# Attention and feed-forward block: every probability unit of query tiles 2 to 7 turned outside TensorE, in pairs, with new instruction orders

## The chip, the cores and the metric

One core of a Trainium2 chip runs the whole program in one launch. The metric is the device time of an execution in microseconds, lower is better. The engines are PE (TensorE, matrix products), DVE (VectorE), ACT (ScalarE), POOL (GpSimd) and SP (SyncE, which here issues all bulk transfers from one queue in order).

## The reference

The input x is 1024 tokens of 512 numbers, all in fp32.

```python
x = x + layernorm(attention(layernorm(x)))
x = x + layernorm(ffn(layernorm(x)))
# attention: 32 query heads, 8 key/value heads of 128, causal, 4 query heads to a key/value head
scores = einsum('bskgd,btkd->bkgst', qh, kh) / sqrt(128); probs = softmax(where(causal, scores, min))
attn = einsum('bkgst,btkd->bskgd', probs, vh);  return attn @ w_dense.T
# ffn: 512 -> 1792 -> 512, silu(g) * u, with activations and weights scaled in blocks of 128
```

## The kernel before

**Precision.** Each fp32 operand of a product is split into a high and a low part (fp32r); `split_passes` gives three passes, high x high, high x low, low x high. The high part is a rounding copy, mostly on ScalarE; the low part is a subtraction, on VectorE or POOL (`lo_part`, `low`).

**Stages.** Values, keys and queries come first (to some 245 us), with the products of two heads at a time in a seven-product scheme (`quad`), and go to scratch in HBM (`k_scr`, `q_scr`, `v_scr`). Then the attention: 8 groups (one key/value head each) of 8 query tiles, so 64 steps t. The order of tiles in a group is 3, 7, 2, 6, 1, 5, 0, 4, so even steps are short tiles (0 to 3) and odd steps long ones (4 to 7). The four query heads are regrouped into four units of 128 rows, each unit holding 32 positions of every head; unit u of tile i sees i * 128 + 32 * (u + 1) keys. Last comes the feed-forward part.

**One step of the attention.** For each unit: scores on PE into one of two PSUM slots (`scores`, item S), scaled and masked maximum on VectorE (`masked_max`, S there), exponential with its sum on ScalarE (`exponentials`, E), reciprocal of the sum on VectorE (`inverse_sum`, E), normalisation on POOL (`norm_head`, E). Then the probabilities have to be turned, keys to the partitions. There are two ways:
- on PE: 128x128 transposes into PSUM (`turn_probs`, item P, line L1920), the high part by ScalarE and the low part by VectorE, both out of PSUM;
- by exchange (`swaps`): SyncE stores a unit in `p_scr` (`swap_away`) and loads it back with its 32-row bands regrouped (`swap_back`, four loads for each unit, in place, all but parts that need not move), VectorE turns 32x32 squares into a buffer `square` (`turn_squares`, T), ScalarE takes the high part and VectorE the low part (H; for unit 3 of tile 7 POOL takes it, HP). Both read SBUF. A unit that goes this way computes its scores with the keys in quarters (runs of 32 keys), for the whole diagonal block, less one block of the upper quarters for units 0 and 1.

Exchanged are, at odd steps 3 to 55, units 1, 2 and 3 of tiles 4, 5 and 6 and all units of tile 7: 87 units. All else is turned on PE.

Then weighted values (`weighted_values`, PV, 3 passes for each block of 128 keys) into one PSUM bank, its high and low part (O, on ScalarE and VectorE), the output share of the group (`output_share`, Y, 12 matmuls) and its addition (A, VectorE). The first weighted sum of a tile waits for all its turned units. Long tiles have one buffer of turned probabilities (`pT`) and one of rows (`probs_long`), short ones likewise (`pT_short`, `probs_short`). `hi_of_swap` waits for the weighted sums of the long tile before.

**What sets the order.** Every engine runs in program order and meets the others at semaphores. The order of the attention's items is written out by `step_items` and `pair_items` and then shifted engine by engine by the tables PE_MOVES, ACT_MOVES, DVE_MOVES, POOL_MOVES and the ..._LATER tables. The queue on SyncE has its own loop; an item in it that waits holds all behind it.

Of the kernel before, what the change touches and what calls it, by code (L numbers as in the profile page):

```python
# [5 lines left out]
F32 = mybir.dt.float32  # L6
# [5 lines left out]
P = 128  # L12
# [8 lines left out]
def sandwich_kernel(nc, x, w_v, w_qk, w_dense, w_up, w_down, s_up, s_down, out):  # L21
# [81 lines left out]

    def low_number(t, u, on_pool):
        units = [w for w in swaps(t) if (w in POOL_LOW[TILES[t]]) == on_pool]
        return low_count(t - 2, on_pool) + units.index(u) + 1

    def low_count(t, on_pool):
        return sum((u in POOL_LOW[TILES[k]]) == on_pool for k in SWAPPED if k <= t for u in swaps(k))

    def step_items(t):
        s, g, items, following, two = t % NT, t // NT, [], t < T - 1, p_banks(t) == 2
        last = g == G - 1
        if t == 0:
            shares = [[], [], [], []]
        elif not two:
            shares = [[], [0], [1], [2, 3]]
        else:
            shares = [[], [0], [1], []] if following else [[], [0, 1], [], [2]]

        if t == T - NT:
            items.append(("zeros",))
        exps = [("E", t + 1, h) for h in range(HG) if following and not swapped(t + 1, h)]
        for h in range(HG):
            items.append(("P", t, 0, h))
            if following and not swapped(t + 1, h):
                items.append(("S", t + 1, h))
            if h >= 1:
                items += exps[:1]
                del exps[:1]  # L130
            items += [("Y", t - 1, head) for head in shares[h]]
            if t == 0 and h == 2:
                items.append(("RQ", 2))
            if t == 1 and h == 0:
                items.append(("RQ", 3))
            if h == 2 and T - NT <= t < T - 2:
                items.append(("RQ", t + 2))
            if not last and s in (4, 5) and h % 2:
                items.append(("RKV", g + 1, (s - 4) * 2 + h // 2))

        if t == 1:
            return items + [("P", t, 1, 0), *exps, ("Y", t - 1, 2), ("P", t, 1, 1), ("Y", t - 1, 3), ("P", t, 1, 2),
                            ("P", t, 1, 3), ("A", t - 1),
                            *[("S", 3, u) for u in swaps(3)]]
        if two:
            if following:
                items += [("P", t, 1, 0), *exps, ("Y", t - 1, 2), ("P", t, 1, 1), ("Y", t - 1, 3),
                          ("P", t, 1, 2), ("PV", t, 0), ("P", t, 1, 3), ("PV", t, 1)]
            else:
                items += [("P", t, 1, 0), ("Y", t - 1, 3), ("P", t, 1, 1), ("P", t, 1, 2), ("PV", t, 0), ("PV", t, 1),  # L150
                          ("P", t, 1, 3)]
        items += exps if not two else []
        if t >= 1:
            items.append(("A", t - 1))
# [1948 lines left out]
```

## Time and profile before

| | |
|---|---|
| runs | 1141.95, 1142.47, 1142.70 us; median 1142.47 |
| profiled execution, first to last instruction (span) | 1140.7 us |
| mean granted TensorE clock | 0.996 |
| runs' median less that span | 1.8 us |
| busy: PE, DVE, POOL, ACT | 1122.7, 833.9, 713.9, 626.1 us |

The profile gives no time of the profiled execution but its span; the runs' median is set against that. Mean durations of single instructions that the prediction uses beside the rows below, in ns: maximum on VectorE of 1024 columns 1219 (896: 1075, 768: 954, 640: 814), its reciprocal 157, its low part out of PSUM of 512 columns 680 (384: 545, 256: 416, 128: 270); on ScalarE the exponential of 1024 columns 1153, the high part out of PSUM of 512 columns 585 (384: 470, 256: 370, 128: 255), out of `square` 1048 for 1024 columns, 939, 839 and 721 for 896, 768 and 640, the query copy of 512 columns with 32-column runs (L1253) 619 and the plain copy `up_hi` 617; on VectorE the squares of 1024, 896, 768 and 640 columns 1233, 1101, 971 and 832 and the low parts out of `square` 1294, 1077, 969 and 914.

How to read it: the busy share of an engine is an average over stages with different limits, so a change is judged in its own stage. The records of some matmuls are missing: 562 of the 582 transposes of the attention are in the trace.

### The profile page before, as it was taken

How to read it: one execution, taken by the hardware profiler on the slowest of the kernel's cores; microseconds unless marked ns; L12 is line 12 of the kernel's file. 1: busy time of each engine (PE TensorE's matmuls, PEld its weight loads, DVE VectorE, ACT ScalarE, POOL GpSimd, SP SyncE). 2: the span in 40 equal slices, each digit the busy share in tenths (PEclk: the TensorE clock that was granted, in tenths of full speed). 3: DMA queues.
4: the chain of work that ended last, by engine and by line, in shares of the span. 5: the costliest groups of instructions: out<-in, count | busy, mean ns of one | idle time of the engine just before them, and what ended most of it. 6: DMA issues, size and time to landing. Idle time of an engine off the chain costs nothing.

```text
span 1140.7 us, 17840 instructions
## 1 busy us (share of the span) xinstructions
PE 1122.7 (98%) x5512; PEld 945.5 (83%) x5512; DVE 833.9 (73%) x1987; ACT 626.1 (55%) x1350; POOL 713.9 (63%) x802
## 2 busy tenths in 40 slices
PE   8999999999999999999999999999999989999997
PEld 7888888888888888888888888888887768888885
DVE  5645454557888898888888888988579766666666
ACT  6532324237776767676767767776588532222224
POOL 7844447436674865856757748567784746665645
PEclk9999999999999999999999999999999999999999
DMA  6443555335466475485474665754410033333422
GB/s 224 138 158 148 184 203 185 148 128 183 129 194 218 152 224 183 142 265 173 143 262 127 206 205 159 240 172 121 167 65 1 20 115 114 109 111 92 121 65 98
DMA packets 154696, 173.76 MB, mean 152 GB/s; under 512 B 41776, under 2 KB 128496, under 8 KB 151280
## 3 DMA queue, kind: packets, MB, share of 16 engines
q1 hardware_dynamic: 154608, 172.68, 46.8%
q8 instruction: 43, 0.70, 0.2%
q14 instruction: 45, 0.37, 0.1%
HBM read 101.06 MB, written 71.57 MB: 151 GB/s over the span
## 4 chain that ended last, share of the span: by engine, by line
PE 93%; DVE 2%; POOL 2%; ACT 1%; issue 1%; DMA 0%; POOLq 0%; DVEq 0%; SPq 0%; ACTq 0%
PE psS L1813 29%; PE psOY L1942 17%; PE psOY L1957 15%; PE psOY L1813 15%; PE psT L1813 11%; PE psT L1920 5%; POOL x L1100 0%; DVE pT_lo L1468 0%; PE psS L1819 0%; POOL raw_up L1000 0%; DMA raw<-in_w_v 0%; DVE y L1612 0%; POOL rstd L1031 0%; POOL up_lo L896 0%; DVE probs_long L1533 0%
## 5 line engine op out<-in xcount | busy, mean ns | idle before, releaser
L955 POOL TENSOR_SCALAR probs_long<-probs_long,rsum 128x896 f32<-128x896 f32 (+9 forms) x124 | 129.0, 1042 | 62.3 <-DVE rsum L1539 60.9
L1269 ACT ACTIVATE probs_long<-probs_long,negmax 128x896 f32<-128x896 f32 (+9 forms) x124 | 121.4, 979 | 42.0 <-DVE negmax L1533 39.7
L955 POOL TENSOR_SCALAR probs_short<-probs_short,rsum 128x416 f32<-128x416 f32 (+15 forms) x128 | 69.0, 543 | 120.1 <-DVE rsum L1539 119.7
L1813 PE MATMUL psS<-kT_hi,qT_hi 128*128 128x256 f32 (+8 forms) x384 | 133.0, 346 | 0.0
L1813 PE MATMUL psS<-kT_hi,qT_lo 128*128 128x256 f32 (+8 forms) x384 | 128.3, 334 | 0.0
L1813 PE MATMUL psS<-kT_lo,qT_hi 128*128 128x256 f32 (+8 forms) x384 | 128.1, 334 | 0.0
L1957 PE MATMUL psOY<-wd_hi,oT_hi 128*128 128x512 f32 x256 | 106.8, 417 | 3.3 <-DVE oT_lo L1468 3.3
L1022 POOL TENSOR_SCALAR hidden<-mask,hr,hs 128x128 f32<-128x128 f32 x112 | 50.0, 456 | 86.2 <-DVE hr L1632 82.1
L1957 PE MATMUL psOY<-wd_hi,oT_lo 128*128 128x512 f32 x256 | 101.2, 395 | 0.0
L1957 PE MATMUL psOY<-wd_lo,oT_hi 128*128 128x512 f32 x256 | 100.5, 393 | 0.0
L1264 ACT CAST pT_hi<-square 128x1024 fp32r<-128x1024 f32 (+3 forms) x87 | 77.6, 892 | 31.6 <-DVE square L1552 31.2
L1942 PE MATMUL psOY<-pT_hi,v_hi 128*128 128x512 f32 x222 | 92.3, 416 | 0.6 <-DVE pT_lo L1468 0.6
L1306 ACT ACTIVATE mask<-psS 128x256 f32<-128x256 f32 x56 | 21.5, 383 | 129.0 <-PE psS L1813 128.9
L1552 DVE STREAM_TRANSPOSE square<-probs_long 128x1024 f32<-128x1024 f32 (+3 forms) x87 | 90.6, 1041 | 0.0
L1813 PE MATMUL psS<-up_hi,xn1T_hi 128*128 128x512 f32 x224 | 88.3, 394 | 2.0 <-DVE xn1T_lo L1468 1.9
L896 POOL TENSOR_TENSOR qT_lo<-q_raw,qT_hi 128x512 fp32r<-128x512 f32 x64 | 82.8, 1294 | 11.5 <-ACT qT_hi L1253 11.5
L1468 DVE TENSOR_TENSOR pT_lo<-square,pT_hi 128x896 fp32r<-128x896 f32 (+3 forms) x81 | 85.4, 1055 | 3.7 <-ACT pT_hi L1264 2.4
L1813 PE MATMUL psS<-up_hi,xn1T_lo 128*128 128x512 f32 x224 | 87.9, 393 | 0.0
L1813 PE MATMUL psS<-up_lo,xn1T_hi 128*128 128x512 f32 x224 | 87.7, 392 | 0.0
L1942 PE MATMUL psOY<-pT_hi,v_lo 128*128 128x512 f32 x222 | 87.2, 393 | 0.0
L1942 PE MATMUL psOY<-pT_lo,v_hi 128*128 128x512 f32 x222 | 86.8, 391 | 0.0
L1533 DVE CUSTOM_DVE_ANT_0 probs_long<-psS,mask 128x1024 f32<-128x1024 f32 (+9 forms) x82 | 83.8, 1024 | 3.2 <-PE psS L1813 2.5
(200 smaller groups left out, 3267.1 us busy)
## 6 DMA issues: line engine op xcount, KB each, us to landing
q_raw<-q_scr SPq DMA_DIRECT2D x64, 256.0 KB, 3.4
p_scr<-probs_long SPq DMA_DIRECT2D x24, 512.0 KB, 3.3
raw<-in_w_qk SPq DMA_DIRECT2D x10, 1024.0 KB, 5.6
p_scr<-probs_long SPq DMA_DIRECT2D x21, 448.0 KB, 2.5
probs_long<-p_scr SPq DMA_DIRECT2D x90, 96.0 KB, 2.8
q_scr<-cB SPq DMA_DIRECT2D x16, 512.0 KB, 2.6
q_scr<-cA SPq DMA_DIRECT2D x16, 512.0 KB, 2.7
raw_wd<-in_w_dense SPq DMA_DIRECT2D x8, 1024.0 KB, 8.4
```

The lines of the kernel that those rows point to most:

```text
L896: return nc.gpsimd.tensor_tensor(dst, source, hi.bitcast(F32), ALU.subtract)
L955: nc.gpsimd.tensor_scalar(row, row, rsum[:, column(t, h)], 1.0, ALU.mult, ALU.mult).then_inc(p_ready, 1)
L1022: last = nc.gpsimd.tensor_scalar(to, columns_of(h_sb[:, m % 2, b * P:(b + 1) * P], to), hr[:, m % 2, b:b + 1], hs[:, m % 2, b:b + 1], ALU. ...
L1264: nc.scalar.copy(pT[0][:, 0:TILES[t] + 1, u * P:(u + 1) * P], squared(t, u)).then_inc(done, 1)
L1269: nc.scalar.activation(row, row, ACT.Exp, bias=negmax[:, column(t, h)], scale=-1.0, accum_out=lsum[:, column(t, h)]).then_inc(e_done, 1)
L1468: return nc.vector.tensor_tensor(dst, source, hi.bitcast(F32), ALU.subtract)
L1533: nc.vector.tensor_tensor_reduce(out=out, in0=scores, in1=keys, scale=-SCALE, scalar=-NEG, op0=ALU.add, op1=ALU.min, accum_out=negmax[:, c ...
L1552: nc.vector.transpose(square[u][:, 0:m * P].rearrange("p (k a q) -> p a k q", k=m, a=HG), whole_row(t, u).rearrange("p (a k x) -> p a k x" ...
L1813: last = nc.tensor.matmul(dst, a, b, start=(start and k == 0), stop=(stop and k == len(terms) - 1), skip_group_check=resumed)
L1920: last = nc.tensor.transpose(bank[:, (j % TPB) * P:(j % TPB + 1) * P], whole_row(t, h)[:, j * P:(j + 1) * P], ident[:])
L1942: last = nc.tensor.matmul(psO, a, b, start=(j == 0 and k == 0), stop=(j == i and k == 2))
L1957: last = nc.tensor.matmul(psY, a, b, start=(h == 0 and k == 0), stop=(h == HG - 1 and k == 2))
```

## The change

1. **More is exchanged.** At all steps 3 to 55, all four units of tiles 2 to 7 are exchanged (156 units); only tiles 0 and 1, and the steps outside that range, are turned on PE. There several units share one turn item (`HEADS`: all four units of tile 0, two of tile 1).
2. **Pairs.** Two units (`PACKS`) lie interleaved in one row and are stored, loaded back (four loads for a pair), turned (in place in `squares`) and rounded by ScalarE together. Loads go to buffers of their own, `squares_long` and `squares_short`, and `p_scr` has two halves. A load back waits for the low parts of the tile of the same length before.
3. **Low parts** go by the table `LOWS` to VectorE (0) or POOL (1).
4. **Normalisation** of units 0 and 2 of tiles 6 and 7 goes to ScalarE; reciprocals are taken for two units at once.
5. **Masks**: one `band` for all units.
6. **q_scr** is laid out by tile, so a load of queries takes pieces of 2 KB instead of 512 B, and a store of queries writes pieces of 512 B instead of 4 KB.
7. **New orders**: for each of the five engines one string of letters (`..._WEAVE`) says which kind of item comes next, over the whole attention and the first steps of the feed-forward part.

```diff
-    SWAPPED = range(3, T - NT, 2)
-    SWAPS = {4: (3, 2, 1), 5: (3, 2, 1), 6: (3, 2, 1), 7: (3, 2, 1, 0)}
...
-    POOL_LOW = {4: (), 5: (), 6: (), 7: (3,)}
...
+    AWAY = range(3, T - NT)
+    PACKS = {0: ((0, 1, 2, 3),), 1: ((0, 1, 2, 3),), 2: ((0, 1), (2, 3)), 3: ((0, 1), (2, 3)), 4: ((0, 1), (2, 3)), 5: ((0, 1), (2, 3)), 6: ((0, 1), (2, 3)), 7: ((0, 1), (2, 3))}
+
+    DVE_LOW, POOL_LOW = 0, 1
+    LOWS = {0: (), 1: (), 2: (((0, 1), 0), ((2, 3), 1)), 3: (((0, 1), 0), ((2, 3), 1)), 4: (((0, 1), 0), ((2,), 0), ((3,), 1)), 5: (((0, 1), 0), ((2,), 1), ((3,), 1)), 6: (((0,), 0), ((1,), 1), ((2,), 0), ((3,), 1)), 7: (((0,), 0), ((1,), 1), ((2,), 0), ((3,), 1))}
+
+    SCALED_BY_ACT = {6: (0, 2), 7: (0, 2)}
+
+    STAYING = (0, 1)
+    HEADS = {0: ((0, 1, 2, 3),), 1: ((0, 1), (2, 3)), 2: ((0,), (1,), (2,), (3,)), 3: ((0,), (1,), (2,), (3,)), 4: ((0,), (1,), (2,), (3,)), 5: ((0,), (1,), (2,), (3,)), 6: ((0,), (1,), (2,), (3,)), 7: ((0,), (1,), (2,), (3,))}
+    def away(t):
+        return t in AWAY and TILES[t] not in STAYING
+
+    def length(t):
+        return int(TILES[t] >= TPB)
...
+    SP_WEAVE = ("qqkqqwqoqoiioqqioiwoqqoiipqpjjqooipipqkjjqooiiqqooiioiqqoi"
...
+    PE_WEAVE = ("psppspssvvvvpspsspspypypvpvpsspvsspvsvvsyypspvssvssvyysyyv"
...
+    SP_ITEMS = woven(SP_KINDS, SP_WEAVE)
+    PE_ITEMS = woven(PE_KINDS, PE_WEAVE)
+    ACT_ITEMS = woven(ACT_KINDS, ACT_WEAVE)
+    DVE_ITEMS = woven(DVE_KINDS, DVE_WEAVE)
+    POOL_ITEMS = woven(POOL_KINDS, POOL_WEAVE)
...
-        square = [at(f"square{u}", 116 + 4 * u, [P, S]) for u in range(HG)]
-        masks = [at(f"mask_{u}", (142, 64, 68)[u], [P, HG, 2 * P]) for u in range(HG - 1)]
+        squares = [at("squares_short", 142, [P, HG * BANK]), at("squares_long", 116, [P, HG * S])]
+        band = at("band", 64, [P, 2 * HG - 1, 2 * P])
...
-        q_scr = nc.dram_tensor("q_scr", [G * HG, P, S], F32, kind="Internal").ap()
+        q_scr = nc.dram_tensor("q_scr", [G, P, NT, HG * P], F32, kind="Internal").ap()
-        p_scr = nc.dram_tensor("p_scr", [HG, P, S], F32, kind="Internal").ap()
+        p_scr = [nc.dram_tensor(f"p_scr_{n}", [2, HG // 2, P, 2 * size], F32, kind="Internal").ap()
+                 for n, size in (("short", BANK), ("long", S))]
...
+            if away(t):
+                k = pack_of(t, u)
+                pack = PACKS[TILES[t]][k]
+                rows = pack_rows(probs_of(t), t, k).rearrange("p (c u x) -> p u c x", c=HG, u=len(pack))
+                return rows[:, u - pack[0]]
...
+            def swap_away(t, k):
+                last = PACKS[TILES[t]][k][-1]
+                if scaled_count(t, last, ON_POOL):
+                    sp.wait_ge(p_ready[lane(t)], scaled_count(t, last, ON_POOL))
+                if scaled_count(t, last, ON_ACT):
+                    sp.wait_ge(p_ready_act[lane(t)], scaled_count(t, last, ON_ACT))
+                rows, c, count = pack_rows(probs_of(t), t, k), length(t), pack_count(t, k)
+                if count > 2:
+                    sp.wait_ge(swap_in[c][k], 16 * HG * (count - 2))
+                sp.dma_start(p_scr[c][count % 2, k, :, 0:rows.shape[1]], rows).then_inc(swap_out[c][k], 16)
+
+            def swap_back(t, k):
+                c, rows = length(t), pack_rows(squares[length(t)], t, k)
+                w = rows.shape[1] // HG
+                sp.wait_ge(swap_out[c][k], 16 * pack_count(t, k))
+                earlier, end = previous(t), PACKS[TILES[t]][k][-1] + 1
+                if earlier >= 0:
+                    sp.wait_ge(swap_lo[c], low_count(earlier, DVE_LOW, end))
+                    if low_count(earlier, POOL_LOW, end):
+                        sp.wait_ge(swap_lo_pool[c], low_count(earlier, POOL_LOW, end))
+                for b in range(HG):
+                    sp.dma_start(rows[b * SPAN:(b + 1) * SPAN, :].rearrange("q (a x) -> q a x", a=HG),
+                                 p_scr[c][pack_count(t, k) % 2, k, :, b * w:(b + 1) * w].rearrange("(a q) x -> q a x", a=HG)
+                                 ).then_inc(swap_in[c][k], 16)
+
+            def store(kind, n, tile, done):
+                if kind == "k":
+                    sp.dma_start(k_scr[n], tile[:]).then_inc(done, 16)
+                else:
+                    sp.dma_start(q_scr[n // HG].rearrange("p n (h c) -> p n h c", h=HG)[:, :, n % HG, :],
+                                 tile[:].rearrange("p (n c) -> p n c", n=NT)).then_inc(done, 16)
...
+            def norm_head(t, u):
+                pool.wait_ge(r_done[lane(t)], pair_count(t, u))
+                row = filled_row(t, u)
+                if u < HG - 1 and away(t - 2) and not away(t):
+                    end = (u + 1) * row_slot(t)
+                    nc.gpsimd.memset(probs_of(t)[:, end - SPAN * (HG - 1 - u):end], 0.0).then_inc(const_ready, 1)
+                nc.gpsimd.tensor_scalar(row, row, rsum[:, column(t, u)], 1.0, ALU.mult, ALU.mult).then_inc(p_ready[lane(t)], 1)
+
+            def lo_of_swap(t, units):
+                pool.wait_ge(swap_hi[length(t)], exchange_count(t, pack_of(t, units[-1])))
+                hi, lo = (turned_units(v_, t, units) for v_ in pT_of(t))
+                low(lo, squared(t, units), hi).then_inc(swap_lo_pool[length(t)], 1)
...
+            def hi_of_swap(t, k):
+                units = PACKS[TILES[t]][k]
+                act.wait_ge(swap_turned[length(t)], exchange_count(t, k))
                 act.wait_ge(o_full, t - 1)
+                nc.scalar.copy(turned_units(pT_of(t)[0], t, units), squared(t, units)).then_inc(swap_hi[length(t)], 1)
...
+            def norm_row(t, u):
+                act.wait_ge(r_done[lane(t)], pair_count(t, u))
+                row = filled_row(t, u)
+                nc.scalar.activation(row, row, ACT.Copy, scale=rsum[:, column(t, u)]).then_inc(p_ready_act[lane(t)], 1)
...
+            def turn_squares(t, k):
+                c = length(t)
+                dve.wait_ge(swap_in[c][k], 16 * HG * pack_count(t, k))
+                rows = pack_rows(squares[c], t, k)
+                rows = rows.rearrange("p (b x) -> p b x", x=SPAN)
+                nc.vector.transpose(rows, rows).then_inc(swap_turned[c], 1)
+
+            def lo_of_swap(t, units):
+                dve.wait_ge(swap_hi[length(t)], exchange_count(t, pack_of(t, units[-1])))
+                hi, lo = (turned_units(v_, t, units) for v_ in pT_of(t))
+                lo_part(lo, squared(t, units), hi).then_inc(swap_lo[length(t)], 1)
...
+                def in_quarters(first, last, blocks, at_):
+
+                    dst = bank[:, at_:at_ + (last - first) * SPAN * blocks].rearrange("p (c k x) -> p c k x", c=last - first,
+                                                                                     x=SPAN)
+                    shown = TILES[t] if first == 2 and u < 2 else blocks
+                    return product(dst[:, :, 0:shown], [(queries, [k_[:, 0:blocks * P].rearrange(
+                        "p (k c x) -> p c k x", c=HG, x=SPAN)[:, first:last, 0:shown] for k_ in kT[e]])])
+
+                if away(t) and n > BANK:
+                    in_quarters(0, 2, TILES[t] + 1, BANK - n // 2)
+                    last = in_quarters(2, HG, TILES[t] + 1, BANK)
+                elif away(t):
+                    last = in_quarters(0, HG, max(TILES[t] + 1, 2), 0)
```

In the new lists PE has 288 transposes instead of 582. Around steps 24 and 25 (a tile 3, then a tile 7) they read, with a unit's number or a pair's last:

```
PE:   PV(24,3) S(28,3) S(29,0) S(29,1) Y(24,0) Y(24,1) Y(24,2) Y(24,3) PV(25,0) PV(25,1)
ACT:  N(27,0) E(27,3) H(25,0) N(27,2) O(24) H(25,1) E(28,0)
DVE:  S(28,3) A(23) O(24) L(25,(0)) L(25,(2)) T(26,0)
POOL: N(27,1) N(27,3) L(25,(1)) L(25,(3)) D(4,0)
```

## Rows read from the trace of the kernel before

**Rows 1.** The head of the page: span, busy time and share of each engine.
```profile
span 1140.7 us, 17840 instructions
...
PE 1122.7 (98%) x5512; PEld 945.5 (83%) x5512; DVE 833.9 (73%) x1987; ACT 626.1 (55%) x1350; POOL 713.9 (63%) x802
...
PE   8999999999999999999999999999999989999997
```

**Rows 2.** The page's chain that ended last, by engine and by line.
```profile
PE 93%; DVE 2%; POOL 2%; ACT 1%; issue 1%; DMA 0%; POOLq 0%; DVEq 0%; SPq 0%; ACTq 0%
...
by line: PE psS L1813 28.5%; PE psOY L1942 17.1%; PE psOY L1957 15.3%; PE psOY L1813 15.1%; PE psT L1813 11.2%; PE psT L1920 5.3%; issue 0.7%; POOL x L1100 0.4%; DVE pT_lo L1468 0.4%; PE psS L1819 0.4%; POOL raw_up L1000 0.4%; DMA raw<-in_w
```

**Rows 3.** Stretches: us, busy PE, PEld, DVE, ACT, POOL, clock, DMA share, GB/s.
```profile
479.71:557.75 78.04, 78.04 (x407) 67.15 (x407) 68.23 (x160) 54.99 (x120) 51.90 (x55) 1.00 0.60 191
```

**Rows 4.** PE's waits from 200 to 900 us: total, times, longest.
```profile
PE psOY L1957 <- DVE oT_lo L1468: 3.3, 3, 2.5
PE psOY L1942 <- DVE pT_lo L1468: 0.6, 2, 0.3
```

**Rows 5.** The chain from 479 to 500 us: start, us, what.
```profile
482.55 0.44 PE psT L1920 x4
...
494.48 2.81 PE psOY L1957 x12
```

**Rows 6.** PE's instructions in order of time: start, us, line, operands.
```profile
480.50 0.40 PE L1813 MATMUL psS<-kT_lo,qT_hi 128*128 128x512 f32 x1
480.73 0.40 PE L1813 MATMUL psS<-kT_hi,qT_lo 128*128 128x512 f32 x1
...
482.39 0.60 PE L1920 MATMUL psT<-ident,probs_short 128*128 128x128 f32 x4
482.74 0.47 PE L1957 MATMUL psOY<-wd_hi,oT_hi 128*128 128x512 f32 x1
483.05 0.39 PE L1957 MATMUL psOY<-wd_lo,oT_hi 128*128 128x512 f32 x1
483.28 0.39 PE L1957 MATMUL psOY<-wd_hi,oT_lo 128*128 128x512 f32 x1
...
497.30 0.34 PE L1813 MATMUL psS<-kT_lo,qT_hi 128*128 128x384 f32 x1
497.48 0.34 PE L1813 MATMUL psS<-kT_hi,qT_lo 128*128 128x384 f32 x1
```

**Rows 7.** Groups by line and shape: count, busy us, mean ns, idle before.
```profile
L1552 DVE STREAM_TRANSPOSE square<-probs_long 128x1024 f32<-128x1024 f32 x24 | 29.6, 1233 | 0.0
L955 POOL TENSOR_SCALAR probs_long<-probs_long,rsum 128x1024 f32<-128x1024 f32 x26 | 29.4, 1129 | 19.6 <-DVE rsum L1539 19.2
...
L1552 DVE STREAM_TRANSPOSE square<-probs_long 128x640 f32<-128x640 f32 x21 | 17.5, 832 | 0.0
...
L896 POOL TENSOR_TENSOR pT_lo<-square,pT_hi 128x1024 fp32r<-128x1024 f32 x6 | 14.5, 2417 | 10.2 <-ACT pT_hi L1264 10.2
```

**Rows 8.** Instructions of POOL, then of VectorE, around 500 us.
```profile
497.31 2.43 POOL L896 TENSOR_TENSOR pT_lo<-square,pT_hi 128x1024 fp32r<-128x1024 f32 x1 [1.71 <-ACT pT_hi L1264]
499.69 1.52 POOL L955 TENSOR_SCALAR probs_short<-probs_short,rsum 128x320 f32<-128x320 f32 x1
...
499.33 1.49 DVE L1468 TENSOR_TENSOR pT_lo<-square,pT_hi 128x1024 fp32r<-128x1024 f32 x1
...
504.65 2.42 DVE L1468 TENSOR_TENSOR pT_lo<-square,pT_hi 128x1024 fp32r<-128x1024 f32 x2
```

**Rows 9.** The groups of the head's copy that waits for its store.
```profile
L1368 ACT COPY cA<-psT 128x512 f32<-128x512 f32 x20 | 11.7, 587 | 43.0 <-PE psT L1813 40.6 <-DMA q_scr<-cA 2.4
```

**Rows 10.** Transfers from 479.71 to 557.75 us: queue share, size, landing.
```profile
q1 hardware_dynamic: 13242, 14.80, 60.0%
...
p_scr<-probs_long SPq DMA_DIRECT2D x4, 512.0 KB, 3.1
...
raw_wd<-in_w_dense SPq DMA_DIRECT2D x1, 1024.0 KB, 8.2
```

More of the change, by code:

```diff
@@ L104, in low_number @@
[L104 to L154, printed above, removed]
-        if t == 0:
-            items.append(("mask",))
-        if last:
-            if not following:
-                items.append(("X", 0))
-        elif s in (4, 6):
-            items.append(("D", g + 1, (s - 4) // 2))
-        items += [("PV", t, j) for j in range(2 if two else 0, TILES[t] + 1)]
-        items.append(("O", t))
-        return items
@@ new lines, in sandwich_kernel @@
+    PLACE = {item: k for units in SOFT for k, item in enumerate(units)}
+    TURNS = [(t, b, heads) for t in range(T) if not away(t) for b in range(TILES[t] // TPB + 1)
+             for heads in HEADS[TILES[t]]]
+    EXCHANGED = [[(t, k) for t in AWAY if away(t) and length(t) == c for k in range(len(PACKS[TILES[t]]))] for c in range(2)]
+    LOW_PARTS = [[[(t, units) for t in AWAY if away(t) and length(t) == c for units, engine in LOWS[TILES[t]] if engine == e]
+                  for e in range(2)] for c in range(2)]
@@ L274, in sandwich_kernel @@
+    ON_ACT = [[(t, u) for t, u in units if away(t) and u in SCALED_BY_ACT.get(TILES[t], ())] for units in SOFT]
+    ON_POOL = [[item for item in units if item not in done] for units, done in zip(SOFT, ON_ACT)]
+    TURN = {("P", *item): k for k, item in enumerate(TURNS)}
     T_ATT = len(TURN)
     assert T_ATT % 2 == 0
[L276 to L277 removed]
@@ L507, in softmax_count, with previous, items, each @@
-    def softmax_count(t, h):
-        return SOFT[t, h] + 1
+    def previous(t):
+        return max((k for k in AWAY if k < t and away(k) and length(k) == length(t)), default=-1)
+    def items(kind, arguments):
+        return [(kind, *args) for args in arguments]
+    def each(kind, count):
+        return [(kind, n) for n in range(count)]
+    QUERIES, PIECES_LATER = range(2, T), [(g, piece) for g in range(1, G) for piece in range(PIECES_KV)]
+    BLOCKS = [(t, j) for t in range(T) for j in range(TILES[t] + 1)]
@@ new lines, in scaled_count, with exchange_count, pack_count, low_count @@
+    def scaled_count(t, u, members):
+        return sum(PLACE[item] <= PLACE[t, u] for item in members[lane(t)])
+    def exchange_count(t, k):
+        return EXCHANGED[length(t)].index((t, k)) + 1
+    def pack_count(t, k):
+        return sum(pack == k and tile <= t for tile, pack in EXCHANGED[length(t)])
+    def low_count(t, engine, before=HG):
+        return sum(tile < t or tile == t and units[0] < before for tile, units in LOW_PARTS[length(t)][engine])
+    def pack_of(t, u):
+        return [u in pack for pack in PACKS[TILES[t]]].index(True)
@@ new lines, in filled_row, with column, score_bank, squared @@
+        def filled_row(t, u):
+            return whole_row(t, u) if away(t) else whole_row(t, u)[:, 0:keys_of(t, u)]
+        def column(t, u, count=1):
+            first = 2 * HG * lane(t) + PLACE[t, u] % (2 * HG)
+            return slice(first, first + count)
+        def score_bank(t, u):
+            return psT[:, PLACE[t, u] % 2, :] if lane(t) else psS[:, PLACE[t, u] % 2, :]
+        def squared(t, units):
+            k = pack_of(t, units[-1])
+            pack = PACKS[TILES[t]][k]
+            blocks = pack_rows(squares[length(t)], t, k).rearrange("p (a u k q) -> p u k a q", a=HG, u=len(pack), q=SPAN)
+            return blocks[:, units[0] - pack[0]:units[-1] + 1 - pack[0]]
```

479 lines of the change are left out of this document (213 added, 266 removed), and 232 rows, old and new, of tables (ACT_LATER, ACT_MOVES, ACT_NORMS, DVE_LATER).

## The prediction

> **What bounds the kernel now.** I read four views, coarse to fine. The head of the page [rows 1] gives the span, 1140.7 us, with PE busy for 98% of it, and PE stands at nine tenths or more in nearly every slice; no other engine passes 73%. The chain of waits shared out by line [rows 2] says the same from the end backwards: 93% of it is PE, and 5.3% of the span is line L1920, the turning of probabilities on TensorE. The stretches [rows 3] show one whole group of the attention, 478 to 558 us, eight query tiles in 78.1 us: PE is busy for all of it at full granted clock, VectorE for 68.2, POOL for 51.9, ScalarE for 55.0. PE's own waits from 200 to 900 us [rows 4] are under 5 us together, and most of that lies after the attention, where the feed-forward begins. So in the attention an instruction taken off PE shortens the program by its own length, until another engine or a transfer is late.
>
> **Prices on PE.** A matmul's "us" in the trace overlaps the next one, so I price by distance from start to start. The chain counts 0.44 us for four turns [rows 5]; the start times say why [rows 6]: 0.35 until the next matmul starts, and this one holds the next back 0.31 where 0.23 is usual. I take 0.108 a turn. A matmul of 512 columns costs 0.231 (three of the output share take 0.69), one of 384 contiguous columns 0.173: 0.455 ns a column. Scores in quarters (runs of 32 keys apart) cost 0.236 at 512 columns: 0.464 ns.
>
> **What PE loses and gains.** Removed: unit 0 of tiles 4, 5 and 6 (7 tiles of each kind between t = 3 and 55, with 5, 6 and 7 blocks: 126 turns) and all four units of tiles 2 and 3 (6 of each, 3 and 4 blocks: 168). 294 turns x 0.108 = 31.8 us. Added: an exchanged unit needs its whole diagonal block. Unit 0 of tiles 4 to 6 goes from 96 missing columns to 64 not shown, so 32 more, x 21 = 672; tiles 2 and 3 get 96+64+32 = 192 more each, x 12 = 2304. 2976 columns x 3 passes x 0.455 = 4.1 us. 36,288 columns change from contiguous to quarters: x 3 x 0.009 ns = 1.0 us. Net **26.7 us**, or 4.7 for a whole group: 73.4 instead of 78.1. Nothing else on PE changes in number; weighted sums and output shares stay.
>
> **What the others must do in 73.4 us**, for one group, from [rows 3, 7] and the durations in the profile section.
> VectorE: turns' low parts go (three long unit 0s 3.3, short ones 4 x (0.545+0.68) = 4.9: -8.2). Squares come: 0.83+0.97+1.10 for the long ones, and from the slope of the rows (1.04 ns a column, 0.16 for the start) 0.56 and 0.70 x 4 for the short ones: +8.0; twelve instructions fewer through pairs, -2.0. Low parts: of 28 units 18 stay here, 11.9 us against 12.8. Sixteen reciprocals fewer, -2.5; wider maxima, +0.8. Together -4.8: 63.4 us, 86%.
> POOL: normalisations of units 0 and 2 of tiles 6 and 7 leave, -4.3; wider rows +0.6; its low parts, 2.417 us for 1024 columns, grow from one unit to ten: 1.5 (tile 4), 3.6 (tile 5), 4.2 (tile 6), 2.4 more (tile 7), 4.2 (tiles 2 and 3): +16.0. 64.2 us, 87% instead of 67%. This is the largest shift of the change.
> ScalarE: high parts out of PSUM -7.1, out of squares +6.9, pairs -2.1, four normalisations +4.1, wider exponentials +0.6: 57.4 us, 78%.
> No one exceeds PE's 73.4, and each has over 9 us of air, against 9.8 on VectorE today. Where squares are turned in place, where ScalarE copies them through runs of 32, and for the band mask, I take today's price. The trace bounds that: query copies of 512 columns with such runs take 619 ns, plain ones 617, so the price is nought, at worst the 0.16 start again for each.
>
> **What is late next.** The lengths of the new lists on PE, priced as above, give the air of each exchange. From the last score of a long tile to its first weighted sum stood 20 to 25 us of other PE work, now 25 (tile 7) to 31 (tile 6); for short tiles 26 and more. The pair's chain is longer: for tile 7 maximum 1.2, exponential 1.15, reciprocal 0.16, normalisation 1.13, out 1 MB 5.6, back 1 MB 5.6 (the page has 5.6 for 1 MB of query weights; half a MB takes 3.1 in rows 10), squares 2.3, high part 1.9, low part 2.4 = 21.5 of 24.9. Tile 5: 18.5 of 26. They fit.
> Tighter is the end of it, where engines stand in order. For tile 7 ScalarE's list reads: output of the tile before, then the high part of the second pair. On PE lie between that output and the first weighted sum one score of tile 1 (0.35), two of tile 5 (1.95) and four output shares (2.8): 5.1 us. Needed are 0.59 (output copy), 1.93 (pair of 1024), VectorE's low part of unit 2 (1.2) and POOL's of unit 3 (2.42), plus 0.1 for handing over. If the two low parts can't run together that is 6.2: 1.1 to 1.2 late. Whether they can the trace shows [rows 8]: POOL's low part ends at 499.74, VectorE's, started at 499.33, takes 1.49 instead of 1.2 (two of them took 2.42), and POOL's next, a normalisation of 320 columns that should take 0.54, takes 1.52 and ends 0.4 after VectorE's. So one waits for the other. Six such tiles: 6.9 us.
> The Trainium skill states this as a rule ("SBUF — State Buffer", section "SBUF: two separate sides"): GpSimd and a VectorE instruction with two SBUF inputs hold the shared port pair in turn, for a whole instruction, and the other fully blocks. The trace agrees; it speaks against the change, for low parts that read PSUM become low parts that read SBUF twice.
> At the other places the order leaves something: after the output of tile 1 come 3.9 us for VectorE's output low part and the pair's low part of tile 5 (1.3+1.9), before tile 3 stand 2.5 us for the output alone (1.3). The output's low part had 1.7 us before its share in the old order and made PE wait 3.3 us in all [rows 4]; it has 1.8 to 3.5 now.
> Before and after: storing queries in pieces of 512 B makes 16 heads' stores slower than 2.7 us, and ScalarE waited 2.4 us for them already [rows 9]; but the copy that waits has 4 us until PE needs its bank, so I cost it nought (at worst 32 x 1 us if that cover were gone). Loading queries in pieces of 2 KB only gets quicker. The new order after tile 55 keeps its instructions apart from joined turns; nought, plus or minus 2 us, by the 3.2 us that PE waits there.
>
> **The sum.** 1140.7 - 26.7 + 6.9 = 1120.9 us of span. The runs' median, 1142.5, lies 1.8 above the profiled span, so the forecast is **1122.7 us**.
>
> **Rivals.**
> (a) No stall: the low parts find their gaps, as they did everywhere today (no PE wait in the groups). For it: rows 4, and what is late once moves the rest later. Then 1142.5 - 26.7 = 1115.8.
> (b) VectorE and POOL become the bound through their common port. In today's group (478 to 558 us) five POOL instructions beside one of VectorE's 12 low parts took 0.5 to 1.0 longer than alone, 3.7 us together (the 320 columns of rows 8 are the first), at 67% load on POOL; at 87%, with POOL instructions of up to 2.4 us, a VectorE low part that finds POOL at work waits 1.2 on average. If half of that (0.6) arrives at PE for each of the 27 long tiles: 16 us, 1131.8. Against it: 9 us of air on each.
> The rule of the skill named above would give this case if the order didn't keep the two apart.
> (c) The other side: the exchange is late. A group's transfers [rows 10] grow from 14.8 MB at 60% to 21.3 MB (28 units out, and whole units back, instead of 13 out and seven eighths back); at today's price a byte that is 0.60 x 21.3/14.8 x 78.0/73.4 = 92%. Pieces of twice the length make it less; how much no row shows for this pattern. Queues lengthen the landings: the 1 MB of dense weights takes 8.2 in this stretch. Tile 7 has 3.4 us to spare over two landings; beyond 7.3 each PE waits, and beyond 9.5 each six tiles eat the 26.7. At 10 each: (20 - 11.2 - 3.4) x 6 = 32, so 1148. On SyncE's queue each load back also stands behind stores that wait for POOL.
>
> **Chances.** Forecast 0.37 (its own range 1119 to 1127), (a) 0.27, (b) 0.20, (c) 0.11, something between (b) and (c) 0.05. Range 1112 to 1139: it holds (a), (b) and half of what is between. A difference of 0.2%, 2.3 us, is about what can be told from none. Faster 0.84, same 0.04, slower 0.12.
>
> **What would show it.** Right: turns on L1920 fall from 582 to 288 in the program and its share of the chain from 5.3% to under 3%; a group takes 73.4 to 75 us; PE idles only before the first weighted sum of tile 7, released by POOL's or VectorE's low part; POOL is busy for 64 us or a little more of it, DMA between 75 and 92%. Wrong: PE waits at many tiles (b), landings over 7 us and PE waits behind squares (c), or a group length under 73, which would mean that a turn costs more than 0.108.

## The result: slower by 56 us, and the profile after

The changed kernel takes 1198.39 us (median of 4 runs, 1194.44 to 1199.78), the kernel before 1142.59 beside it: a ratio of 1.0482, 95% interval 1.0465 to 1.0499. The forecast of 1122.7 missed by 76 us and the range ended at 1139. The profiled execution spans 1195.7 us.

The page of the changed kernel: head, DMA share in slices, and the chain that ended last by engine and by line. They answer to [rows 1] and [rows 2].
```profile
PE 1117.8 (93%) x5218; PEld 928.2 (78%) x5218; DVE 862.6 (72%) x1698; ACT 640.3 (54%) x1237; POOL 804.1 (67%) x836
...
PE 54%; DMA 17%; DVE 13%; issue 5%; POOL 4%; ACT 3%; SPq 3%; DVEq 0%; POOLq 0%; ACTq 0%
PE psS L1586 16%; PE psOY L1586 14%; PE psT L1586 11%; DMA squares_long<-p_scr_long 10%; PE psOY L1719 7%; DMA p_scr_long<-probs_long 6%; PE psOY L1734 5%; DVE pT_lo L1242 4%; SPq L497 2%; DVE squares_long L1329 2%; PE psT L1700 2%; POOL pT_lo L662 1%; DVE probs_long L1310 1%; POOL probs_long L722 1%; DVE y L1387 1%
```
Two things show here. PE has 294 matmuls fewer, as forecast, and the chain is no longer PE's: 46% of it is transfers, VectorE and others. (All turns are in both traces, 582 before and 288 now. The 562 named in the section on the profile before leave out 20 that read `probs_mid`.) No engine is above 72% but PE.

Two stretches of one group each (columns as in [rows 3]): 85.7 and 85.8 us, where the old order took 78.1 and 73.4 were forecast.
```profile
345.83:431.53 85.70, 78.75 (x370) 65.50 (x368) 71.53 (x122) 59.02 (x107) 66.97 (x61) 0.98 0.87 255
431.53:517.32 85.79, 77.34 (x354) 64.09 (x354) 71.17 (x121) 56.47 (x103) 66.49 (x62) 0.96 0.84 248
```
The transfers of the first of them (queue: packets, MB, share; then size and landing); they answer to [rows 10].
```profile
q1 hardware_dynamic: 10318, 21.80, 86.5%
...
squares_long<-p_scr_long SPq DMA_DIRECT2D x8, 256.0 KB, 7.2
q_raw<-q_scr SPq DMA_DIRECT2D x8, 256.0 KB, 6.5
p_scr_long<-probs_long SPq DMA_DIRECT2D x2, 1024.0 KB, 7.6
...
raw_wd<-in_w_dense SPq DMA_DIRECT2D x1, 1024.0 KB, 8.8
```
What waited for what from 250 to 930 us: total, times, longest. The two waits of PE in [rows 4] made 3.9 us together:
```profile
DVE squares_long L1329 <- DMA squares_long<-p_scr_long: 62.9, 37, 3.7
PE psS L1586 <- DVE negmax L1310: 40.3, 20, 4.7
PEld psS L1586 <- issue: 34.0, 14, 4.9
PEld psS L1586 <- DVE negmax L1310: 16.8, 18, 2.1
PEld psOY L1734 <- DVE oT_lo L1242: 13.3, 14, 3.0
```
(PEld is the loading of weights on TensorE. Its rows tell much of the same idle time again and aren't to be added: before the score at 443.88 PE idles 2.75 us for negmax, and its weight load 2.93 us as "issue".) PE hardly waits for turned probabilities: by the same view 2.7 us for POOL's low parts and 0.6 for VectorE's. It waits for the masked maximum (negmax), that is for a free score bank: VectorE, which must free the bank, stands in its list behind squares that haven't landed. The chain shows the link (start, us, what), one for each group:
```profile
422.88 7.10 DMA p_scr_long<-probs_long
...
431.53 9.58 DMA squares_long<-p_scr_long
441.13 1.89 DVE squares_long L1329
...
446.39 3.40 DVE pT_lo L1242
```
At that place, VectorE's instructions, then POOL's, then PE's in order of time:
```profile
436.87 2.31 DVE L1329 STREAM_TRANSPOSE squares_long<-squares_long 128x2048 f32<-128x2048 f32 x1 [3.10 <-DMA squares_long<-p_scr_long]
...
441.13 2.31 DVE L1329 STREAM_TRANSPOSE squares_long<-squares_long 128x2048 f32<-128x2048 f32 x1 [1.45 <-DMA squares_long<-p_scr_long]
443.37 0.35 DVE L1310 CUSTOM_DVE_ANT_0 probs_short<-psS,mask 128x224 f32<-128x224 f32 x1
...
445.26 4.54 DVE L1242 TENSOR_TENSOR pT_lo<-squares_long,pT_hi 128x1024 fp32r<-128x1024 f32 x2
...
445.47 3.24 POOL L662 TENSOR_TENSOR pT_lo<-squares_long,pT_hi 128x1024 fp32r<-128x1024 f32 x1 [0.20 <-ACT pT_hi L1031]
...
443.88 0.42 PE L1586 MATMUL psS<-kT_hi,qT_hi 128*128 128x384 f32 x1 [2.75 <-DVE negmax L1310]
...
446.86 0.63 PE L1734 MATMUL psOY<-wd_hi,oT_hi 128*128 128x512 f32 x1
447.28 0.63 PE L1734 MATMUL psOY<-wd_lo,oT_hi 128*128 128x512 f32 x1
...
448.14 0.40 PE L1734 MATMUL psOY<-wd_hi,oT_hi 128*128 128x512 f32 x1
448.38 0.40 PE L1734 MATMUL psOY<-wd_lo,oT_hi 128*128 128x512 f32 x1
```
VectorE idles 3.10 and then 1.45 us for the two pairs of tile 7; the small maximum at 443.37 comes only after the second, and PE starts at 443.88 after 2.75 us of nothing. Then two low parts of 1024 columns take 4.54 us on VectorE, beside one of 3.24 on POOL (2.417 in [rows 7]). The last lines, of TensorE's clock, are read in the last section.

So two suspects stand: the transfers (rival c of the prediction) and the port that VectorE and POOL share (rival b). Before the experiments the first was the theory (called T), the second the rival (E, the engines), with the in-order lists (O) as a third.

### The profile page after: what moved, and what is told of

It is laid out like the page before. It is cut to its first block, busy times and chain, and to the rows that moved or that the text cites. A ratio compares the mean times of both kernels' runs of the same rounds, so it can differ in the third digit from the quotient of the medians.

```text
span 1195.7 us, 16875 instructions
## 1 busy us (share of the span) xinstructions
PE 1117.8 (93%) x5218; PEld 928.2 (78%) x5218; DVE 862.6 (72%) x1698; ACT 640.3 (54%) x1237; POOL 804.1 (67%) x836
## 4 chain that ended last, share of the span: by engine, by line
PE 54%; DMA 17%; DVE 13%; issue 5%; POOL 4%; ACT 3%; SPq 3%; DVEq 0%; POOLq 0%; ACTq 0%
PE psS L1586 16%; PE psOY L1586 14%; PE psT L1586 11%; DMA squares_long<-p_scr_long 10%; PE psOY L1719 7%; DMA p_scr_long<-probs_long 6%; PE psOY L1734 5%; DVE pT_lo L1242 4%; SPq L497 2%; DVE squares_long L1329 2%; PE psT L1700 2%; POOL pT_lo L662 1%; DVE probs_long L1310 1%; POOL probs_long L722 1%; DVE y L1387 1%
## 5 line engine op out<-in xcount | busy, mean ns | idle before, releaser
L1586 PE MATMUL psS<-kT_hi,qT_hi 128*128 128x384 f32 (+6 forms) x384 | 140.5, 366 | 40.6 <-DVE negmax L1310 40.3
L1329 DVE STREAM_TRANSPOSE squares_long<-squares_long 128x1792 f32<-128x1792 f32 (+3 forms) x54 | 102.2, 1893 | 62.9 <-DMA squares_long<-p_scr_long 62.9
L722 POOL TENSOR_SCALAR probs_long<-probs_long,rsum 128x768 f32<-128x768 f32 (+9 forms) x98 | 93.2, 961 | 67.5 <-DVE rsum L1317 67.4
L662 POOL TENSOR_TENSOR pT_lo<-squares_long,pT_hi 128x896 fp32r<-128x896 f32 (+3 forms) x47 | 108.7, 2322 | 42.6 <-ACT pT_hi L1031 42.4
L1586 PE MATMUL psS<-kT_hi,qT_lo 128*128 128x384 f32 (+6 forms) x384 | 134.2, 349 | 0.0
L1586 PE MATMUL psS<-kT_lo,qT_hi 128*128 128x384 f32 (+6 forms) x384 | 134.0, 349 | 0.0
L1586 PEld LDWEIGHTS psS<-kT_hi,qT_hi 128*128 128x128 f32 x384 | 75.6, 197 | 58.1 <-issue 34.0
L1031 ACT CAST pT_hi<-squares_long 128x1792 fp32r<-128x1792 f32 (+3 forms) x54 | 84.9, 1572 | 47.9 <-DVE squares_long L1329 47.6
L1242 DVE TENSOR_TENSOR pT_lo<-squares_long,pT_hi 128x896 fp32r<-128x896 f32 (+4 forms) x47 | 105.3, 2257 | 0.2 <-ACT pT_hi L1031 0.2
L722 POOL TENSOR_SCALAR probs_short<-probs_short,rsum 128x512 f32<-128x512 f32 (+13 forms) x128 | 70.2, 559 | 35.7 <-DVE rsum L1317 35.6
```

Of the source, the lines that this page charges most:

```text
L662: return nc.gpsimd.tensor_tensor(dst, source, hi.bitcast(F32), ALU.subtract)
L722: nc.gpsimd.tensor_scalar(row, row, rsum[:, column(t, u)], 1.0, ALU.mult, ALU.mult).then_inc(p_ready[lane(t)], 1)
L1031: nc.scalar.copy(turned_units(pT_of(t)[0], t, units), squared(t, units)).then_inc(swap_hi[length(t)], 1)
L1242: return nc.vector.tensor_tensor(dst, source, hi.bitcast(F32), ALU.subtract)
L1329: nc.vector.transpose(rows, rows).then_inc(swap_turned[c], 1)
L1586: last = nc.tensor.matmul(dst, a, b, start=(start and k == 0), stop=(stop and k == len(terms) - 1), skip_group_check=resumed)
```

## The experiments

Each starts from the changed kernel unless said otherwise. Steps up to 10, that is the first 92 us of the attention, stay whole in all edits "from step 11 on"; what is lost there stays in. Ratios are to the kernel before, run beside each (1142.3 to 1143.6).

**1. A quarter of each band, out and back.** From step 11 on only the first quarter of each run is stored and loaded; the rest of the squares is stale.
```diff
-sp.dma_start(p_scr[c][count % 2, k, :, 0:rows.shape[1]], rows).then_inc(swap_out[c][k], 16)
+w = rows.shape[1] // HG
+x_ = w if t <= 10 else w // 4
+sp.dma_start(p_scr[c][count % 2, k, :, 0:rows.shape[1]].rearrange("p (b x) -> p b x", b=HG)[:, :, 0:x_],
+             rows.rearrange("p (b x) -> p b x", b=HG)[:, :, 0:x_]).then_inc(swap_out[c][k], 16)
... (the load back likewise)
```


> The changed kernel, but from step 11 on each store of a pair and each load back moves only a quarter of every band (the rest of the buffers keeps old data); all instructions, waits and orders stay. Theory T (transfers): the exchange's bytes, 21 MB a group at a DMA share of 0.87, make the landings long (9.5 us from issue for a pair of tile 7) and these hold the chain; with a quarter of the bytes landings fall below 3 us, a group to 73 to 76 us and the program to 1116 to 1135. Rival O (order and buffers): the waits come from the order of the queue and from single buffers, whatever the bytes; then it stays above 1160. Rival E (VectorE and POOL, with their waits for one another): above 1175.

Measured: 1158.16 us, ratio 1.0134 (1.0097 to 1.0171). 40 us come back. The theory of the transfers had 1116 to 1135 and each of its rivals more than 1160, so none holds alone: the transfers are the larger part, and some 15 us of slowdown have another cause.

**2. A quarter of the loads back only** (the stores whole; same edit in the load alone).


> The changed kernel, but from step 11 on only the loads back move a quarter; stores are whole. T: 37% fewer bytes in the exchange and the last landing short: 1120 to 1150, most of the way of the run with both in quarters. O: above 1165. E: above 1175.

Measured: 1160.66, ratio 1.0156 (1.0108 to 1.0204). With only half of the bytes saved it is 2.5 us slower, which two runs of each (1157.1 and 1159.2, 1158.9 and 1162.5) don't clearly tell apart. Three kernels over the same stretch, 425 to 680 us (after, loads a quarter, both a quarter):
```profile
425.00:680.00 255.00, 229.21 (x1057) 190.91 (x1056) 211.48 (x350) 166.97 (x300) 193.89 (x178) 0.97 0.83 250
```
```profile
425.00:680.00 255.00, 240.77 (x1151) 203.16 (x1150) 233.40 (x388) 183.20 (x330) 206.82 (x191) 0.99 0.57 190
```
```profile
425.00:680.00 255.00, 242.39 (x1171) 204.35 (x1170) 234.60 (x396) 186.37 (x336) 209.87 (x193) 1.00 0.42 113
```
From a DMA share of 0.83 to 0.57 nearly all is gained, from 0.57 to 0.42 almost nothing. The kernel before ran at 0.60 [rows 3].

**3. Short low parts.** From step 11 on the low parts of exchanged units cover one block instead of all, on VectorE and on POOL; the transfers stay whole.
```diff
-hi, lo = (turned_units(v_, t, units) for v_ in pT_of(t))
+m = TILES[t] + 1 if t <= 10 else 1
+hi, lo = (turned_units(v_, t, units)[:, :, 0:m] for v_ in pT_of(t))
... (squared(t, units) is cut to [:, :, 0:m] likewise)
```


> The changed kernel, but from step 11 on the low parts of exchanged units, on VectorE and on POOL, cover one block of 128 keys instead of all (the weighted sums then use stale low parts); this takes some 11 us a group from VectorE, 16 from POOL, and nearly all their waits for one another. T: the landings stay, so 1170 to 1195. E: 1115 to 1150.

Measured: 1167.64, ratio 1.0217 (1.0178 to 1.0256). This is outside both expectations: 31 us come back with every byte still moved. So neither cause alone gives the 56. As the low parts' own work is left out with their conflict, this run can't tell the two apart; runs 6, 7 and 9 do.

**4. The old layout of the query scratch** (whole heads stored, queries loaded in runs of 512 B).


> The changed kernel with the queries' scratch laid out by head as before (stores of 4 KB pieces, loads of 512 B pieces). ScalarE waited 34 us for the stores in the first stage of the changed kernel against 2.4 before, yet the first weighted sum starts at 257.4 against 257.6 us. Expected: ScalarE's wait back to some 3 us and the first weighted sum within 1 us of 257; the loads of queries cost more engine time in the attention, so no gain: 1194 to 1205. If the layout mattered for the total: below 1185.

Measured: 1194.66, ratio 1.0454 (1.0409 to 1.0498), which can't be told from the change. The wait of ScalarE for the heads' stores did grow, from 2.4 us [rows 9] to 34.1, and is back at 2.4 here, without effect on the time, as the prediction had it: the first weighted sum starts at 257.4 us in the changed kernel, at 257.2 here and at 257.6 before.

**5. Both: a quarter of the bytes and short low parts.**


> The changed kernel from step 11 on with both relieved at once: only a quarter of each band is stored and loaded back (as in the quarter run before), and the low parts of exchanged units cover one block instead of all (as in the run with short low parts); both leave out part of the computation. Alone they took 38 and 31 us off 1198.4. Theory T+E (two limits, the transfers and VectorE/POOL, that hide each other; the order of the lists is sound): with both gone the saving on PE comes through, 1112 to 1125. Rival A (the in-order lists make waits of their own, whatever the durations): it stays near what the quarter gave, 1145 to 1158. Rival B (both took the same us away, there is one limit): 1150 or more as well, with VectorE idle at loads.

Measured: 1123.59, ratio 0.9826 (0.9807 to 0.9845). With both limits gone the saving on TensorE comes through. Two starts of the first square of tile 7 on VectorE, one group apart, and the stretch between them:
```profile
427.74 2.31 DVE L1334 STREAM_TRANSPOSE squares_long<-squares_long 128x2048 f32<-128x2048 f32 x1
```
```profile
501.39 2.31 DVE L1334 STREAM_TRANSPOSE squares_long<-squares_long 128x2048 f32<-128x2048 f32 x1
```
```profile
427.74:501.39 73.65, 73.65 (x361) 63.12 (x360) 59.75 (x123) 56.75 (x106) 48.27 (x62) 1.00 0.44 120
```
A group takes 73.65 us with PE busy throughout; forecast were 73.4. The order of the lists is sound: rival A of this run falls. (The saving of the whole run, 18.7 us, is short of 26.7 by what the whole part before step 11 loses; see below.)

**6. A quarter, and only POOL's low parts short. 7. A quarter, and only VectorE's short.**


> Quarter bands as before, and of the low parts only those on POOL are short (VectorE's are whole). If VectorE's waits at the port shared with POOL are what is left after the transfers (its low parts of 1024 took 1.8 to 2.4 us beside POOL's), this gives most of the both-short run: 1120 to 1135. If it is VectorE's own work, nothing comes of it: 1150 to 1158.

> Quarter bands, and only VectorE's low parts are short (POOL's whole, up to 3.3 us each). If VectorE's own load or its port waits are what is left: 1125 to 1140, near the both-short run. If POOL's length is what PE waits for: 1145 to 1158.

Measured: 1126.74, ratio 0.9851 (0.9832 to 0.9871), and 1136.94, ratio 0.9950 (0.9932 to 0.9968). Taking POOL's instructions away frees VectorE. VectorE's low parts from 430 to 850 us by shape, in the run of the quarter (1), then with POOL's short (6), then VectorE's own short ones beside POOL's whole ones (7):
```profile
L1246 DVE TENSOR_TENSOR pT_lo<-squares_long,pT_hi 128x896 fp32r<-128x896 f32 x10 | 25.5, 2576 | 0.0
L1246 DVE TENSOR_TENSOR pT_lo<-squares_long,pT_hi 128x1024 fp32r<-128x1024 f32 x10 | 23.8, 2417 | 0.0
L1246 DVE TENSOR_TENSOR pT_lo<-squares_long,pT_hi 128x1536 fp32r<-128x1536 f32 x5 | 17.1, 3429 | 0.0
```
```profile
L1247 DVE TENSOR_TENSOR pT_lo<-squares_long,pT_hi 128x1024 fp32r<-128x1024 f32 x10 | 13.6, 1396 | 0.0
L1247 DVE TENSOR_TENSOR pT_lo<-squares_long,pT_hi 128x896 fp32r<-128x896 f32 x10 | 11.8, 1207 | 0.0
L1247 DVE TENSOR_TENSOR pT_lo<-squares_long,pT_hi 128x1536 fp32r<-128x1536 f32 x5 | 9.6, 1925 | 0.0
```
```profile
L1246 DVE TENSOR_TENSOR pT_lo<-squares_long,pT_hi 128x128 fp32r<-128x128 f32 x25 | 31.6, 1284 | 0.8 <-ACT pT_hi L1035 0.8
```
The same instruction of 896 columns takes 2.58 us beside POOL's and 1.21 without them, and one of 128 columns still takes 1.28, against 0.39 where POOL's are short too (run 5): its length is no longer its work but what is left of POOL's instruction. The three shapes above lose 13.7 + 10.2 + 7.5 = 31 us in these 420 us, 5.9 for a group of 79.

**8. Units one by one instead of by pairs**, same bytes and orders (the item lists are unfolded to single units).


> The changed kernel with the same orders and the same bytes, but units exchanged, squared, turned and split one by one instead of by pairs: transfers of 512 KB instead of 1 MB, twice as many, and about 60 more instructions a group on VectorE, ScalarE and POOL together. If the length of the chain behind one pair (store, then load, 7 to 10 us each) is what makes PE wait, it gains: 1165 to 1190. If the share of bytes in the group is (0.85 of all DMA engines), the time stays or grows: 1190 to 1215.

Measured: 1207.84, ratio 1.0566 (1.0534 to 1.0599). The landings get shorter (loads back 4.1 us instead of 7.2), the DMA share stays at 0.81 over 425 to 680 us, and the time grows by 9. Shorter single landings alone give nothing back, and the pairs are worth keeping. What the 60 more instructions a group cost was not measured, so they may hide a small gain.

**9. The port by itself.** As 1, but from step 11 on each of VectorE's low parts is replaced by turning the same squares in place again: the same columns, one input from SBUF instead of two, POOL's work whole. These low parts are left out.
```diff
-lo_part(lo, squared(t, units), hi).then_inc(swap_lo[length(t)], 1)
...
+    for u in range(len(units)):
+        again = squared(t, units)[:, u]
+        last = nc.vector.transpose(again, again)
+    last.then_inc(swap_lo[length(t)], 1)
```


> Quarter bands, POOL's low parts whole, and each of VectorE's low parts of exchanged units (two inputs from SBUF) replaced by turning the same squares in place once more: the same columns, one input from SBUF, about the same length alone (1.04 ns a column and 0.16 for the start). The low parts are left out of the result. If what is left after the transfers is the port that VectorE and POOL share, which only an instruction with two inputs would have to wait for, this gives what short parts on POOL gave: 1125 to 1135. If it is the amount of work on VectorE and its order, it stays at 1150 to 1158.

Measured: 1126.09, ratio 0.9858 (0.9835 to 0.9880). VectorE's replaced instructions, then POOL's low parts, which were 2376 ns for the same shape in run 1, and one group:
```profile
L1343 DVE STREAM_TRANSPOSE squares_long<-squares_long 128x896 f32<-128x896 f32 x10 | 10.7, 1093 | 0.0
```
```profile
L666 POOL TENSOR_TENSOR pT_lo<-squares_long,pT_hi 128x896 fp32r<-128x896 f32 x10 | 21.1, 2135 | 0.1
```
```profile
427.87:501.65 73.78, 73.78 (x360) 63.03 (x360) 64.51 (x125) 56.77 (x106) 60.66 (x62) 1.00 0.44 120
```
VectorE and POOL have all their columns here and a group takes 73.78 us. VectorE's replaced instructions are a little shorter than its low parts undisturbed (1093 ns against the 1207 of run 6), too little to account for 5 us a group. So the amount of work was not the trouble; the conflict of two-input instructions on VectorE with POOL's was, and it costs 1158.2 - 1126.1 = 32 us beside short transfers. The Trainium skill ("SBUF — State Buffer", section "Who interferes with whom") states just this pair: a VectorE instruction with two SBUF inputs contends with a GpSimd instruction that reads SBUF, one with at most one input doesn't. Runs 6, 7 and 9 agree.

**10. The kernel before with two more units exchanged** (unit 0 of tiles 5 and 6, in its table of exchanged units only).
```diff
-SWAPS = {4: (3, 2, 1), 5: (3, 2, 1), 6: (3, 2, 1), 7: (3, 2, 1, 0)}
+SWAPS = {4: (3, 2, 1), 5: (3, 2, 1, 0), 6: (3, 2, 1, 0), 7: (3, 2, 1, 0)}
```


> The kernel before with unit 0 of tiles 5 and 6 exchanged as well, by its own single-unit exchange and its own order rules: 7 x (6+7) = 91 turns less on TensorE, 9.8 us by the price of 0.108, 0.9 back for the columns; transfers from 14.8 to about 17.2 MB a group, which is 0.60 to about 0.70 of the DMA engines; the low parts of the new units on VectorE, POOL's share unchanged. If the exchange pays as long as neither the transfers nor the port are the limit: 1130 to 1137. If already the next units make PE wait: 1141 or more.

Measured: 1302.83, ratio 1.1399 (1.1368 to 1.1430), a plain miss. DMA share is only 0.51 over 340 to 730 us and the landings are the old ones (512 KB in 3.1 us), so it says nothing of either limit. PE waits for VectorE's maxima and output parts, each a little:
```profile
PEld psS L1813 <- DVE negmax L1533: 41.6, 35, 3.6
PEld psOY L1957 <- DVE oT_lo L1468: 39.0, 15, 3.8
```
The hand-set offsets of that order count items, and with more items the lists slip against each other. That this costs the 160 us is argued from these waits and the code, not tested.

**11. The kernel before with filler traffic.** After each of its 87 exchanges back SyncE's queue also copies 512 KB from memory to memory, for nobody.
```diff
+sp.dma_start(fill[len(fills)], k_scr[7]).then_inc(fill_done, 16)
```


> The kernel before with a filler on SyncE's queue: after each of its 87 exchanges back, a copy of 512 KB from memory to memory that nobody reads, about 13 a group, 6.7 MB: the group's 14.8 MB become 21.5, as in the changed kernel, and nothing else changes. If a share of 0.85 to 0.9 of the DMA engines by itself makes the exchanges late, it slows down: 1155 to 1190. If bytes cost only where the chain of a pair is long, it stays within 1140 to 1150.

Measured: 1189.45, ratio 1.0410 (1.0385 to 1.0435). The stretch of [rows 3], and the store of [rows 10] over 425 to 595 us:
```profile
479.71:557.75 78.04, 71.40 (x357) 59.27 (x356) 61.63 (x138) 50.20 (x105) 44.00 (x45) 1.00 0.80 250
```
```profile
p_scr<-probs_long SPq DMA_DIRECT2D x8, 512.0 KB, 4.5
```
Added traffic alone slows the old kernel by 47 us: at a share of 0.80 instead of 0.60 the store of half a megabyte lands after 4.5 us instead of 3.1.

**12. Filler beside a short exchange.** Run 9 with two such copies after each exchange back from step 11 on.


> The kernel of the last but two runs (quarter bands, VectorE's low parts with one input, 1126.1 us) and a filler: after each exchange back from step 11 on two copies of 512 KB from memory to memory that nobody reads, some 24 a group, so that the DMA engines are as full as in the changed kernel (0.8 to 0.9) while the exchange's own transfers stay at a quarter of their bytes. If what makes PE wait is how full the DMA engines are (every transfer lands late), it loses most of the 40 us again: 1150 to 1175. If it is the length of the exchange's own transfers, 1126 to 1138.

Measured: 1191.58, ratio 1.0429 (1.0409 to 1.0450), 65 us more than run 9 and above the range given. Over 425 to 850 us, and two landings over 425 to 595 us:
```profile
425.00:850.00 425.00, 382.96 (x1778) 322.52 (x1777) 318.76 (x610) 278.89 (x504) 293.23 (x292) 0.96 0.76 244
```
```profile
squares_long<-p_scr_long SPq DMA_DIRECT2D x16, 64.0 KB, 3.2
p_scr_long<-probs_long SPq DMA_DIRECT2D x4, 256.0 KB, 6.1
```
A store of 256 KB took 2.7 us in run 9 and takes 6.1 here. So traffic beside them makes even short transfers late, and their own size isn't needed for it. But the path is another than in the changed kernel. From 425 to 850 us:
```profile
ACT qT_hi L1030 <- DMA q_raw<-q_scr: 32.4, 12, 6.7
DVE squares_short L1339 <- DMA squares_short<-p_scr_short: 15.1, 9, 3.8
DVE squares_long L1339 <- DMA squares_long<-p_scr_long: 10.4, 12, 3.1
```
In the changed kernel VectorE waits 46.1 us for long squares over this stretch, and ScalarE only 2.9 for queries. The share isn't the whole measure either: at 0.76 the filler costs 65 us, where the changed kernel's own traffic, at 0.82 over the same stretch, costs 40 by run 1. What stays open: the filler is issued on SyncE's queue as everything else, and it reads and writes the memory, so runs 11 and 12 don't part full engines from a full queue or a busy memory; and no version that computes everything and beats the kernel before was found.

## Why the prediction was wrong, step by step

- **TensorE's saving, -26.7 us: right.** 294 matmuls fewer, 288 turns left, the turns' share of the chain 2%, and 73.65 us a group (73.4 forecast) where nothing is late. The 4.7 us for a whole group don't follow from the prices beside them: 46 turns, 480 columns and the quarters make 4.2, or 73.9; the sum of 26.7 is not touched.
- **What the engines have to do: right as work, wrong as time.** Forecast were 63.4 for VectorE, 57.4 for ScalarE and 64.2 for POOL; with no port conflict (run 9) they are busy for 64.5, 56.8 and 60.7. In the changed kernel it is 71.5, 59.0 and 67.0. "Each has over 9 us of air" counted an instruction at its length alone. The unit counts are wrong as written, though the times beside them come out: tiles 2 to 7 have 24 units a group, not 28, of which `LOWS` gives 13 to VectorE and 11 to POOL, not 18 and ten.
- **The port: the mechanism named, its term mis-sized.** I priced 1.15 us at the end of tile 7 only, 6.9 in all, and gave rival (b) 16 us. Removed on top of the quarter bands it gives 32; removed alone (run 3, with the work itself gone too) 31. The step that failed is that the conflict mattered only where the lists gave too little air: the low parts of all 24 units a group now have two SBUF inputs, and the conflict spreads over them (5.9 us a group on VectorE in run 1).
- **"They fit": the step that failed first.** The two landings of tile 7's pair were taken at 5.6 us each; they took 7.6 and 7.2 by the median of a stretch, 9.4 to 10 us for the load in the five longest pieces of the chain. Rival (c) had the mechanism and the traffic (21.3 MB forecast, 21.8 measured), at a chance of 0.11. I set 92% beside "landings" but kept 5.6 us, a load of the first stage, where the DMA share up to 258 us is 0.47, though [rows 10] had 1 MB landing after 8.2 us within the attention. The price per microsecond failed as well: by the prediction's own formula 7.6 and 7.2 are 0.2 us beyond the air of 14.6, which makes 1 us over six tiles, and 7.1 and 9.6 as in the chain make 13, against the 40 that run 1 gives back. The reason is where the wait lands: not at the weighted sum of the late tile, where I counted air, but in VectorE's list, behind which stand the maxima of other tiles, and so PE's next scores.
- **The two add up.** Alone, run 1 gives back 40.2 us and run 3 gives back 30.8, together 71.0; both at once, run 5, give 74.8. In run 5 the early, whole part still keeps PE idle for 5.6 us from 258 to 350 and 3.4 up to 427.74; without these its span of 1123.0 would be 1114.0, the span of rival (a). The stall of 6.9 us that I added doesn't show there, but run 5 has no long low parts; run 9, with POOL's whole and no conflict, has PE busy for all of its 73.78 us too.
- **First stage and queries: right**, costed at nought; run 4 shows it.

## What to carry to other kernels

When a change moves more bytes through the same DMA engines, take the landing times from a stretch that is as full as the new one will be, not from today's; here a share of 0.57 to 0.60 cost little or nothing and 0.83 cost 40 us. When work shifts to instructions with two SBUF inputs on VectorE while POOL is busy too, price each at its own length plus what is left of POOL's. And look for a late transfer's price in what stands behind it in the waiting engine's list, rather than at the consumer it was meant for.

## What the runs showed of the hardware

- A subtraction of 128 columns on VectorE took 1.28 us on average beside POOL's low parts, about as long as one of 896 without them (1.21). POOL loses as well: 2376 ns for 896 columns beside VectorE's, 2135 where those have one input.
- A landing depended more on the traffic than on its size: 256 KB out took 2.7 us at a share of 0.44 (run 9, 425 to 595 us) and 6.1 at 0.78 (run 12, same stretch).
- Waiting costs TensorE twice. It pauses for 1.55 us before 439.46 and for 2.75 before 443.88. After the second pause the granted clock is still 1.00 from 443.88 to 444.50, then 0.50 from 445 to 448.14 while PE is busy throughout, and 1.00 again after it. At 0.50, the lower of its two levels (1.2 GHz), matmuls of 512 columns start 0.42 us apart (446.86 to 447.28), and from 448.14 again 0.24. The granted clock of the group is 0.96 to 0.98. From 436.87 to 778.88 us, four groups, PE is busy for 310.23 us, where run 5 needs 294.62 for its four (427.74 to 722.36): of the 47.4 us lost in these groups 15.6 are matmuls that take longer, and the other 31.8 are idle time.
